# Convolution stage: three taps by TensorE with diagonal matrices, and the rescaling of x by ScalarE in front of each step

## What is computed

```python
xc = conv_general_dilated(transpose(x), dw_kernel, padding=(2, 0), feature_group_count=D) + dw_bias   # 3 causal taps, one filter per channel
xc = silu(einsum('bdl,ed->bel', xc, pw_w) + pw_b)
x1 = x + transpose(xc)
logits = x1 @ router_w.T + router_b                      # 8 experts, the top 2 weighted by a softmax
ye = silu(einsum('bsd,eod->bseo', x1, expert_w) + expert_b)
combined = einsum('bse,bseo->bso', rw, ye)
h = norm_w * rms_normalised(x1 + combined @ out_w.T + out_b)
ff = gelu(h @ ff_down_w.T + ff_down_b) @ ff_up_w.T + ff_up_b
x = layernorm(x + h + ff)
```

## Time and profile before

| | |
|---|---|
| time, median of 3 runs (lowest to highest) | 3258.83 us (3252.49 to 3266.7) |
| the profiled execution's own time | 3253.52 us |
| its span, from the first to the last instruction | 3251.8 us |
| the stage of the change in it | about 2343.0 to 2488.8 us: 146 us, 4.5% of the span |
| busy in the stage (2343 to 2489): PE, DVE, ACT, POOL | 83.28, 108.22, 46.34, 63.29 us |
| mean granted TensorE clock, whole span (1.0 is 2.4 GHz, 0.5 is 1.2 GHz) | 0.912 |
| the same in 2343 to 2411, 2411 to 2440, 2440 to 2489 | 0.73, 0.68, 0.60 |

### The profile page before, as it was taken

How to read it: one execution, slowest core, us unless ns; L and a number is a source line. 1 busy time by engine, 2 the same in 40 slices (tenths; PEclk the granted TensorE clock), 3 DMA queues, 4 the chain that set the end, 5 groups by cost and what they waited for, 6 DMA issues and landing times. The chain is left out here.

```text
span 3251.8 us, 44820 instructions
## 1 busy us (share of the span) xinstructions
PE 2725.2 (84%) x16256; PEld 1271.1 (39%) x16256; DVE 2036.4 (63%) x4829; ACT 1339.1 (41%) x2299; POOL 962.9 (30%) x1206
## 2 busy tenths in 40 slices
PE   4998778978875988998988999968863999698997
PEld 1332334433322443454563444443431233254555
DVE  4884772159996755666784655656576876573444
ACT  1665553256552551221213433425641667263221
POOL 3111200048895101333342555552044110200000
PEclk9998789988877899999999999997875999698999
DMA  4220310000002300122230000003001220420000
GB/s 126 42 45 32 67 19 20 0 1 0 1 0 74 72 19 6 41 50 54 50 70 19 1 1 1 1 3 65 14 0 22 43 42 16 101 42 1 1 1 14
DMA packets 45655, 95.71 MB, mean 29 GB/s; under 512 B 14246, under 2 KB 33498, under 8 KB 39598
## 3 DMA queue, kind: packets, MB, share of 16 engines
q1 hardware_dynamic: 43708, 90.96, 12.8%
q10 hardware_dynamic: 1728, 1.89, 0.3%
HBM read 46.20 MB, written 1.38 MB: 15 GB/s over the span
## 5 line engine op out<-in xcount | busy, mean ns | idle before, releaser
L1819 POOL TENSOR_TENSOR mamba_dbu<-mamba_du,mamba_b 128x512 f32<-128x512 f32 x128 | 244.4, 1909 | 41.1 <-DVE stream L1849 12.3
L1849 DVE TENSOR_TENSOR_SCAN stream<-mamba_da,mamba_dbu 128x512 f32<-128x512 f32 x128 | 216.7, 1694 | 17.1 <-issue 11.9
L1579 PE MATMUL ps<-stream,weights 128*128 128x512 f32 x256 | 157.9, 727 | 58.8 <-DVE stream L1859 43.1
L559 DVE TENSOR_REDUCE L0a_negmax<-ps 128x1 f32<-128x512 f32 x256 | 162.4, 683 | 50.1 <-PE ps L302 49.7
L559 DVE TENSOR_REDUCE L3a_negmax<-ps 128x1 f32<-128x512 f32 x256 | 162.4, 683 | 49.8 <-PE ps L302 49.4
L2681 DVE TENSOR_REDUCE skv_negmax<-ps 128x2 f32<-128x1024 f32 (+3 forms) x128 | 101.1, 798 | 129.8 <-PE ps L2524 129.8
L405 ACT ACTIVATE L0a_probs<-ps 128x512 f32<-128x512 f32 x256 | 143.5, 599 | 76.3 <-PE ps L321 74.5
L405 ACT ACTIVATE L3a_probs<-ps 128x512 f32<-128x512 f32 x256 | 143.7, 600 | 74.1 <-PE ps L321 72.6
L2743 ACT ACTIVATE skv_probs<-ps 128x1024 f32<-128x1024 f32 (+3 forms) x128 | 90.1, 704 | 187.0 <-PE ps L2550 187.0
L164 POOL TENSOR_SCALAR vareps<-mv 128x4 f32<-128x4 f32 x24 | 9.8, 410 | 508.3 <-DVE mv L1319 508.1
L189 PE MATMUL ps<-stream,xT 128*64 128x512 f32 x512 | 129.3, 623 | 12.8 <-DVE moa_v L2306 6.6
(11 more groups left out here) (624 smaller groups left out, 6581.9 us busy)
## 6 DMA issues: line engine op xcount, KB each, us to landing
moa_masks<-picked SPq DMA_DIRECT2D x32, 512.0 KB
stream<-stream SPq DMA_DIRECT2D x28, 192.0 KB
stream<-gate_up_down_in SPq DMA_DIRECT2D x1, 4352.0 KB, 17.2
stream<-value_output_in SPq DMA_DIRECT2D x1, 4096.0 KB, 12.0
moa_gateb<-gates SPq DMA_DIRECT2D x32, 128.0 KB
stream<-ffn_in SPq DMA_DIRECT2D x1, 2888.0 KB, 9.9
L0a_qs<-L0a_qs SPq DMA_DIRECT2D x16, 128.0 KB
L0x_qs<-L0x_qs SPq DMA_DIRECT2D x16, 128.0 KB
```

What stands on the lines that cost most here:

```text
L559: dve.tensor_reduce(negmax[:, hh // G % 4, a, hh % G:hh % G + 1], ps[:, i % S_RING, :], AX.X, ALU.max, negate=True).then_inc(s["maxed"], 1)
L1579: pe.matmul(ps[:, SUM_BANK + j, :], k.ident, hc[:, (J * i + j) % RING, :], start=n == 0, stop=n == N - 1).then_inc(s["summed"], 1)
L1819: pool.tensor_tensor(dbu[:, m % RING, :], du[:, b % 2, j, :], bsb[:, i % B_RING, :], ALU.mult).then_inc(s["dbu_ready"], 1)
L1849: dve.tensor_tensor_scan(out=hs[:, m % RING, :], data0=da[:, m % RING, :], data1=dbu[:, m % RING, :], initial=0.0, op0=ALU.mult, op1=ALU.a ...
```

## The change

Two edits in `conv_experts`.

The convolution: ahead of step 0 DVE builds `conv_taps`, three 128x128 diagonal matrices (identity times one column of filter weights). In each step 0 to 3 PE does three products of 128x512, 128x511 and 128x510 with them, which add up in PSUM bank A, ahead of the first piece of `experts` (which belongs to the batch before). ACT copies the sum with the bias to `conv_acc` (`copy_convolved`), behind `copy_x1` and ahead of the first `silu`. DVE's three instructions go.

The rescaling: POOL computes `conv_offset` = -(mean times rstd) with two small instructions behind `inverse_deviation` (`shift`), and ACT does the four instructions of 128x128 (`rescale_x`) at the very head of the next step, ahead of `copy_mix` and `copy_h`. DVE's four instructions go. `add_out` waits for the rescaling of the batch before, which reads the same `k.resid`.

```diff
@@ conv_experts, buffers
+        taps = sb("taps", [P, TAPS, P])
+        offset = sb("offset", [P, NT])
@@ PE
+                def convolve(b):
+                    if b == 0:
+                        pe.wait_ge(s["taps_ready"], TAPS)
+                    take(A_BANK, "conv_done", b + 1)
+                    for back in range(TAPS):
+                        last = pe.matmul(ps[:, A_BANK, back:], taps[:, back, :], k.xTs[:, b, 0:SEQ - back], start=back == 0,
+                                         stop=back == TAPS - 1, skip_group_check=True)
+                    last.then_inc(s["conv_ready"], 1)
...
                     if batch(J, 4) is not None:
                         down(batch(J, 4))
+                    if batch(J, 0) is not None:
+                        convolve(batch(J, 0))
                     if batch(J, 1) is not None:
                         experts(batch(J, 1), 0, 3)
@@ ACT
+                def copy_convolved(b):
+                    act.wait_ge(s["conv_ready"], b + 1)
+                    if b:
+
+                        act.wait_ge(s["pw_ready"], b)
+                    act.activation(acc[:, :], ps[:, A_BANK, :], ACT.Identity, bias=W("cb")).then_inc(s["conv_done"], 1)
...
+                def rescale_x(b):
+                    act.wait_ge(s["offset_ready"], b + 1)
+                    for t in range(NT):
+                        last = act.activation(k.xs[:, b, t, :], k.resid[:, t, :], ACT.Identity, bias=offset[:, t:t + 1],
+                                              scale=k.rstd[:, t:t + 1])
+                    last.then_inc(s["x_ready"], 1)
...
                 for J in range(BATCH + OFFSETS - 1):
+                    if batch(J, 5) is not None:
+                        rescale_x(batch(J, 5))
                     if batch(J, 3) is not None:
                         copy_mix(batch(J, 3))
                     if batch(J, 4) is not None:
                         copy_h(batch(J, 4))
                     if batch(J, 1) is not None:
                         copy_x1(batch(J, 1))
+                    if batch(J, 0) is not None:
+                        copy_convolved(batch(J, 0))
+                    if batch(J, 1) is not None:
                         silu(batch(J, 1), 0, 3)
@@ DVE
-                def convolve(b):
-                    x = k.xTs[:, b, :]
-                    chain(dve.tensor_scalar(acc[:, :], x, W("conv")[:, TAPS - 1:TAPS], W("cb"), ALU.mult, ALU.add))
-                    for back in range(1, TAPS):
-                        last = dve.scalar_tensor_tensor(out=acc[:, back:], in0=x[:, 0:SEQ - back],
-                                                        scalar=W("conv")[:, TAPS - 1 - back:TAPS - back], in1=acc[:, back:],
-                                                        op0=ALU.mult, op1=ALU.add)
...
                 def add_out(b):
                     dve.wait_ge(s["up_ready"], b + 1)
                     dve.wait_ge(s["hb_ready"], b + 1)
+                    if b:
+
+                        dve.wait_ge(s["x_ready"], b)
...
+                for back in range(TAPS):
+                    dve.tensor_scalar(taps[:, back, :], k.ident, W("conv")[:, TAPS - 1 - back:TAPS - back], None, ALU.mult
+                                      ).then_inc(s["taps_ready"], 1)
                 for J in range(BATCH + OFFSETS - 1):
                     if batch(J, 4) is not None:
                         scale_h(batch(J, 4))
-                    if batch(J, 0) is not None:
-                        convolve(batch(J, 0))
-                    if batch(J, 5) is not None:
-                        rescale(k, dve, s, batch(J, 5))
@@ POOL
+                def shift(b):
+                    chain(pool.tensor_tensor(offset[:, :], k.mv[:, :, 0], k.rstd[:, :], ALU.mult))
+                    pool.tensor_scalar(offset[:, :], offset[:, :], -1.0, None, ALU.mult).then_inc(s["offset_ready"], 1)
+                    pool.wait_ge(s["offset_ready"], b + 1)
...
                     if batch(J, 4) is not None:
                         inverse_deviation(k, pool, s, batch(J, 4))
+                        shift(batch(J, 4))
```

More of the change, by code:

```diff
@@ L2833, in batch @@
             return J - offset if 0 <= J - offset < BATCH else None
-        with phase(k, "chain", "pool_chain", "conv_done", "pw_ready", "pw_sb", "x1T_done", "logits", "logits_read", "turned",
+        with phase(k, "chain", "pool_chain", "taps_ready", "conv_ready", "conv_done", "offset_ready", "pw_ready", "pw_sb", "x1T_done", "logits", "logits_read", "turned",
                    "x1_sb", "e_in", "ye_in", "ye_out", "e_out", "e_exp", "rw_ready", "x1b_ready", "half_ready", "comb_ready",
@@ L3003, in scale_h @@
                     last.then_inc(s["h_ready"], 1)
-                def convolve(b):
-                    x = k.xTs[:, b, :]
-                    chain(dve.tensor_scalar(acc[:, :], x, W("conv")[:, TAPS - 1:TAPS], W("cb"), ALU.mult, ALU.add))
-                    for back in range(1, TAPS):
-                        last = dve.scalar_tensor_tensor(out=acc[:, back:], in0=x[:, 0:SEQ - back],
-                                                        scalar=W("conv")[:, TAPS - 1 - back:TAPS - back], in1=acc[:, back:],
-                                                        op0=ALU.mult, op1=ALU.add)
-                        if back < TAPS - 1:
-                            chain(last)
-                    last.then_inc(s["conv_done"], 1)
                 def route(b):
```

## The result

Over 19 runs of each, the changed kernel takes 3264.82 us (median; 3257.72 to 3271.92) and the kernel before 3256.39 us (3251.57 to 3266.7). The ratio is 1.0019, 95% interval 1.0011 to 1.0027, which is +6.2 us (3.6 to 8.8); the two medians as they stand differ by 8.4 us. The forecast was 3266 us and +7.5.

What follows compares the result with a forecast made beforehand. Taken as bounds: TensorE's experts' products from step 1, VectorE in step 2, a long dependency chain per batch in steps 5 to 8. 4.0 - 5.9 + 2.6 + 6.8 = +7.5 us on 3258.8 gave 3266 us, range 3251 to 3281.

Steps and rivals of the forecast that it cites:

- Head, steps 0 and 1: Stage's first two steps: later pointwise and added taps, partly repaid by an earlier full clock; +4 us, bounds +3.2 and +7.4.
- a half clock in step 1: Sign named in advance that the forecast would be wrong: TensorE's clock at half in the stage's second step.
- Step 2: VectorE-bound step: routing starts 3.3 us earlier, taps hide in TensorE's idle, last products gain 2.6; -5.9 us, other bound -3.3.
- step 2 gives nothing: Rival, chance 0.10: GpSimd's mixing still sets routing's end and the clock falls as before; +13.4 us, 3272 us.
- Step 3: Taps of batch 3 stand ahead of the experts' products VectorE waits for; +2.6 us, up to +5.4 if the clock rises late.
- Step 4: Step of the stage that has neither edit; 0 us.
- Tail: Steps 5 to 8: rescaling at the head of ScalarE's list delays the copies and products behind it; +6.8 us, lower bound +4.5.
- step 7: Tail: rescaling, copy_h and down delay turn_x, so add_out moves by +1.7 us.
- step 8: End of the tail: rstd to x takes 2.3 us in place of 1.15; +1.1 us.
- the tail hides: Rival, chance 0.14: ScalarE's queue is not what project and down wait for; +1.8 us, 3261 us.
- The clock's rival: Rival, chance 0.06: clock stays at half through steps 0 and 1; +17.2 us in the head, +20.7 in all, 3280 us.
- VectorE was not the bound: Answers the rival, chance 0.03, that VectorE was the bound after all and its removed work shortens the kernel; -20 us, 3239 us.

Runs made afterwards that it cites:

- e1: Changed kernel with the rescaling back on VectorE, so only the convolution taps on TensorE; whole time no different from the kernel before, tail 49.48 us.
- e3: Changed kernel with ScalarE's rescaling moved behind its two copies, copy_mix and copy_h; tail 49.25 us, as before the change.
- e7: Changed kernel with the tap group of batch 2 computed twice, six more TensorE records; step 2 took 15.80 us, 0.9 more than in the changed kernel.
- e8: Changed kernel plus two unread 128x512 products behind pointwise of step 0; steps 0 and 1 took 24.72 us in place of 25.50.
- e6: Kernel before with VectorE's convolution of batch 2 moved to the end of step 1; ratio 1.0004, stage 144.04 us.
- e4: Changed kernel with taps on TensorE for batch 2 alone, other convolutions and all rescaling on VectorE; ratio 0.998 to the kernel before, stage 142.97 us.
- e10: Repeat of the kernel before with VectorE's convolution of batch 2 moved to the end of step 1; ratio 1.0002, stage 141.11 us.
- e12: The kernel before, unchanged, profiled a second time; 3258.74 us, stage 146.02 us.
- e2: Changed kernel with all convolutions back on VectorE, so only the rescaling on ScalarE; ratio 1.0031 to the kernel before, tail 56.07 us.
- e5: Taps on TensorE for batch 2 alone; ScalarE rescales batches 0 to 2 behind its copies, VectorE batch 3; ratio 1.0001 to the kernel before, stage 140.74 us.
- e9: Repeat of the kernel with batch 2's taps on TensorE and batches 0 to 2 rescaled behind ScalarE's copies; ratio 0.9990 to the kernel before, stage 140.70 us.

## Why the prediction was right

**Head, steps 0 and 1: +4 forecast, +4.75 measured.** `pointwise(0)` came 3.67 us later, forecast 3.9: the right mechanism and size (4.5 to 4.6 in e1, e3 and e7). The taps of batch 1 were taken warm, 2.6 us, and took 4.43, 4.53 and 4.58 in three kernels; e8 shows that they take 2.74 when TensorE does not wait in front of them. I had let the clock rise once and stay up; a half clock in step 1 was one of the signs by which I would have been wrong, and it was there for 4 us. That the sum held is in part luck: in the profile shown the clock was still full for routing's products, which brought back 1.2 us in place of the 0.5 I had put down. In e1, e3 and e7, which have the same steps 0 and 1, it was not, and these steps took 6.9 to 7.1 us more than before's 20.75, near my upper bound of +7.4.

The table load ran from 2354.85 to 2356.13, 0.01 us behind the function before it, and the next function started at 2356.15, 0.07 us behind the end of `pointwise` (2354.98 + 1.10): hidden, as taken from the earlier trace rows. The drain of 1.38 us that the Trainium skill ("ScalarE: Activation LUTs", "What ACT_TABLE_LOAD costs") adds to each switch is not in this trace: the next function started 0.02 us behind the load.

**Step 2: -5.9 forecast, -6.8 measured.** The direction and the first cause were right, the parts were not. From the start of `conv_x1T` to routing on VectorE it was 6.84 us and is 3.47: -3.4, forecast -3.3. Routing itself, which I had left at 7.35 us, took 5.24: -2.1 (5.2 in e1 and e6, but 6.5 in e4; what sets it is open). The products and bias sums behind it, up to `conv_comb`, took 6.19 us and not 7.48: -1.3, where I had put -2.6 for the full clock. Two wrong sizes of opposite sign made up the sum. The clock's share does not need the taps: the eight records behind the wait took 5.40 us in e6 and 3.71 in e10, one kernel without any taps on TensorE, and 3.70 in e4 with them. The rival that step 2 gives nothing is out. That before's own step 2 varies from 18.75 to 21.67 us (e12) means that two profiles cannot size this term. Over three profiles with VectorE's convolution (before, e12, e2) and three with all the taps (changed, e1, e3) the means differ by +5.7 in steps 0 and 1, -5.9 in step 2, +2.2 in step 3: +1.7 for the whole head, where the two profiles shown have -0.3 and the forecast +0.7.

**Step 3: +2.6 forecast, +1.9 measured. Step 4: 0, and -0.2.** In step 3 part of the tap group, 3.66 us, ran half cold, but the experts' six records behind it took 2.74 in place of 4.35.

**Tail: +6.8 forecast, +7.3 measured.** Step 5 +1.0 (forecast 1.0), step 6 +2.9 (3.0), step 7 +2.35 (1.7), step 8 +1.1 (1.1). In step 7 the last `up` took 2.07 us at the lower clock (1.15 before), a term that I had left alone. e2 gives the tail's loss to the rescaling, and e3 gives it to the place in the queue: the same instructions behind the copies cost nothing but step 8's 1.1. The rival "the tail hides" is out, and with it VectorE's 3.98 us in step 5: taking them away only made it wait.

**The whole.** The terms add up to +7.0 us in the stage, and the two profiles differ by that. The ratio says +6.2 (3.6 to 8.8), and the forecast of +7.5 lies inside. With the means of three profiles the stage would have lost 9.0 us, so the closeness of 7.0 to 7.5 is better than the readings are. The 3266 us, too, stand on a median before of 3258.83 from three runs; over 19 it is 3256.39. The clock's rival (+17 in the head) was not met: the clock did fall in step 1, but for 4 us. VectorE was not the bound: about 20 us of its work went and the kernel became slower.

**What stays open.** e5, e9, e6 and e10 have stages 4 to 7 us shorter than before's 148.00, and their whole times say +1 to -3 us. Part is that 148.00 itself is high: e12 had 146.02. Part is the clock: over 175 runs of the study, each taken as its difference from its own kernel's mean, time and mean granted clock are correlated with r = -0.74, at -1.4 us per +0.001 of clock; against before's mean on the same chip (0.9130 for e5 and e6, 0.9122 for the others) e5 had 0.9111, e6 0.9105, e9 0.9119 and e10 0.9110, by an estimate at that rate worth 0.4 to 3.5 us. Whether these programs get a lower clock through something they do, or by chance, no run here tells; e4, at 0.9140, has the best time, and its repeat, at 0.9119, the lesser one, so a part of e4's 6.5 us may be the clock's too. e4's edit was faster in both of its sets, by 0.20% and by 0.08%, the second with an interval that reaches 1; that more of it can be had is not shown.

## What to carry to other kernels

Work moved to another engine costs, besides its duration, what stands behind it in that engine's list: an instruction that waits for a late result belongs behind those whose input is early, and its order is worth trying before its engine (e3: 7 us for the same instructions). Take away from an engine only where the timeline shows others waiting for it (step 2), and leave it where they don't: the same edit paid in one step of four. When a stage's edit is worth 0.2% of a kernel, profile the kernel before twice, so that the scatter of its terms is known before they are explained.

## What the runs showed of the hardware

- The granted clock fell within one step: full in 2353 to 2355, 0.51 in 2361 to 2363, full again in 2363 to 2365, behind waits of 0.87 and 1.54 us with short products between. Four records of unread filler in that place brought the six behind them from 4.43 to 2.74 us.
- The same instructions in the same order had heads of 98.60, 100.13 and 100.33 us, and stages of 148.00 and 146.02 us. The last stage took 256.0 to 259.5 us by dips of the clock that came and went between executions of one kernel.
- Four activations of 128x128 on ScalarE with both bias and scale from pointers took 1.65 to 1.66 us in the steps shown; VectorE's four took 1.11 us alone and 3.06 to 3.98 beside GpSimd. On its own engine the work is steadier, but not shorter in the last step.
